# Normalising three layers by row tile and by half rows, the last layer's end written into both branches of a four-layer graph network

## The reference, cut to what matters

```python
edge_index = jnp.stack([src, dst])
x = _layernorm(x + _L0_gnn_ref(...))   # two RGCN layers, 3 relations, each with a gate over 8 x 64 query rows
x = _layernorm(x + _L1_gnn_ref(...))   # GCN: sum of (x @ W) over the edges, by degree, + b
x = _layernorm(x + _L2_gnn_ref(...))   # two RGAT layers with attention, 4 heads and 1 head
x = _layernorm(x + _L3_gnn_ref(...))   # RGCN with 34 relations, then a GCN: h1 @ W_gcn over the edges, + b_gcn

def _layernorm(x, axis=-1, eps=1e-05):
    m = jnp.mean(x, axis=axis, keepdims=True)
    v = jnp.var(x, axis=axis, keepdims=True)
    return (x - m) / jnp.sqrt(v + eps)
```

## Time and profile before

| | us |
|---|---|
| three timed runs | 1088.4, 1088.81, 1089.32 (median 1088.81) |
| the profiled execution | 1089.91 |
| its span, from the first to the last instruction | 1088.2 |
| its mean granted TensorE clock | 0.994 of full speed |
| TensorE busy | 1039.5 (96%) |
| VectorE busy | 764.1 (70%) |
| ScalarE busy | 573.4 (53%) |
| GpSimd busy | 263.4 (24%) |

### The profile page before, as it was taken

The page is one execution under the profiler, slowest core; times in us unless marked ns, Lnnn a source line. Parts: engine busy times, 40 slices in busy tenths (PEclk is TensorE's granted clock), DMA queues, the critical chain, the costliest instruction groups (busy, mean ns, idle before and its releaser), DMA issues.

```text
span 1088.2 us, 17713 instructions
## 1 busy us (share of the span) xinstructions
PE 1039.5 (96%) x7444; PEld 858.3 (79%) x7444; DVE 764.1 (70%) x1092; ACT 573.4 (53%) x606; POOL 263.4 (24%) x160
## 2 busy tenths in 40 slices
PE   6999999999999999999999989989999999999987
PEld 5889986454699984455879689956999999999974
DVE  8793855888654238887644584745989998989862
ACT  0432226888533248887324363324667676766630
POOL 3524705999300038996100000000000000000000
PEclk9999999999999999999999999999999999999999
DMA  8043247212043373220424302604978787877830
GB/s 296 12 135 129 88 149 230 59 59 59 2 174 123 119 220 130 60 59 20 160 88 175 117 1 87 246 11 138 304 256 283 256 284 256 270 261 263 276 118 29
DMA packets 82291, 163.18 MB, mean 150 GB/s; under 512 B 4044, under 2 KB 60136, under 8 KB 81918
## 3 DMA queue, kind: packets, MB, share of 16 engines
q1 hardware_dynamic: 80736, 151.86, 41.4%
q0 software_dynamic: 1472, 10.15, 3.4%
HBM read 158.35 MB, written 0.80 MB: 146 GB/s over the span
## 4 chain that ended last, share of the span: by engine, by line
PE 80%; DVE 13%; issue 4%; ACT 2%; POOL 1%; DVEq 0%; POOLq 0%; ACTq 0%
PE PS L1089 20%; PE PS L770 8%; PE PS L941 7%; PE PS L786 5%; PE PS L692 5%; PE PS L581 4%; PE PS L1072 4%; PE PS L511 4%; PE PS L668 4%; PE PS L524 3%; PE PS L593 3%; PE PS L1105 2%; PE PS L1006 2%; PE PS L828 2%; DVE PRD L1677 1%
## 5 line engine op out<-in xcount | busy, mean ns | idle before, releaser
L1926 DVE TENSOR_TENSOR Wlo<-W,Whi 128x2304 fp32r<-128x2304 f32 x68 | 172.1, 2551 | 19.0 <-ACT Whi L1425 19.0
L1425 ACT CAST Whi<-W 128x2304 fp32r<-128x2304 f32 x68 | 144.5, 2127 | 0.2 <-DMA W<-in_L_rel 0.2
L1089 PE MATMUL PS<-Whi,Mhi 128*128 128x384 f32 x408 | 138.0, 338 | 0.0
L1089 PE MATMUL PS<-Wlo,Mhi 128*128 128x384 f32 x408 | 136.5, 335 | 0.0
L1089 PE MATMUL PS<-Whi,Mlo 128*128 128x384 f32 x408 | 136.5, 334 | 0.0
L478 POOL TENSOR_TENSOR PRDP<-arena 128x1024 f32<-128x1024 f32 x48 | 114.8, 2391 | 30.1 <-issue 17.9
L770 PE MATMUL PS<-QH,SEL 128*128 128x512 f32 x384 | 115.7, 422 | 5.3 <-ACT xT L1262 1.4
L1283 ACT ACTIVATE arena<-PS 128x1024 f32<-128x1024 f32 x96 | 98.4, 1025 | 23.6 <-PE PS L770 23.5
L770 PEld LDWEIGHTS PS<-QH,SEL 128*128 128x128 f32 x384 | 64.8, 188 | 55.2 <-DVE PRD L1677 21.3
L1283 ACT ACTIVATE PS<-PS 128x1024 f32<-128x1024 f32 x96 | 97.9, 1019 | 2.6 <-PE PS L770 2.6
L1089 PEld LDWEIGHTS PS<-Whi,Mhi 128*128 128x128 f32 x408 | 76.8, 188 | 0.4 <-DVE Wlo L1926 0.2
(11 more groups left out here) (296 smaller groups left out, 2430.3 us busy)
## 6 DMA issues: line engine op xcount, KB each, us to landing
W<-in_L_rel SPq DMA_DIRECT2D x68, 1152.0 KB, 6.4
W<-in_W_rel SPq DMA_DIRECT2D x6, 2304.0 KB, 9.3
W<-in_W SPq DMA_DIRECT2D x6, 2304.0 KB, 9.4
arena<-in_qU SPq DMA_DIRECT2D x96, 128.0 KB, 2.6
W<-in_WqT SPq DMA_DIRECT2D x4, 2304.0 KB, 9.7
W<-in_W_root SPq DMA_DIRECT2D x2, 2304.0 KB, 13.5
W<-in_WgT SPq DMA_DIRECT2D x2, 2304.0 KB, 9.7
QH<-QH POOLq DMA_DIRECT2D x2, 1536.0 KB, 9.9
```

Source lines behind the costliest of these rows:

```text
L1089: mm = pe.matmul(PS[:, 4 + s % 2, 0:HALF], MS[a][mb][:, k, j * P:(j + 1) * P], WS[b][w % 3][:, k, :], start=n == 0, stop=n == 17)
L1425: nc.scalar.copy(WS[0][w % 3][:], W[(FIRST34 + r) % 2][:, :, q * HALF:(q + 1) * HALF]).then_inc(w_hi, 1)
L1926: V.tensor_tensor(WS[1][w % 3][:], W[(FIRST34 + r) % 2][:, :, q * HALF:(q + 1) * HALF], WS[0][w % 3][:].bitcast(F32), ALU.subtract).then_i ...
```

## The change

1. `norm_x`, `normalise`: normalisations 2, 3 and 4 go by row tile. `normalise_tile(n, t)` makes mean and variance of one tile, waits for ScalarE's root of that tile (128x1 in place of 128x2), and scales that tile. It stands right behind the statistics of its tile. Normalisation 1 keeps its form as `normalise_first`. The counts that engines wait for follow.
2. `gcn_out` adds the results of layers 1 and 3 by half rows: `natural` tells `rows_done` after each of its first three halves, VectorE adds one half (128x384) and takes its statistics. `row_stats` goes.
3. The rows are turned tile by tile: tile 0 right behind the product (after 4 warm-up products in layer 1, none in layer 2), then 16 warm-up products, then tile 1. Before, 26 and 18 stood ahead of both. After layer 2 the turned rows go to banks 4 to 6 in place of 0 to 2.
4. The end of layer 3 (`last_product` on TensorE, `last_rows` on VectorE) is written into both branches in place of once behind them. ScalarE's end stays behind its branches.
5. ScalarE takes a square root of `eps` into an unused tile `eps_sd`, ahead of its wait for the turned counts.

```diff
-            def natural(bank, T, Wm, first=True, last=True, ready=None, tile_sem=None):
+            def natural(bank, T, Wm, first=True, last=True, ready=None, half_sem=None):
                 for t in range(NT):
-                    if t and tile_sem:
-                        mm.then_inc(tile_sem, 1)
                     for h in range(2):
+                        if half_sem and (t, h) != (0, 0):
+                            mm.then_inc(half_sem, 1)
...
-            def to_turned(bank, N, ready=None):
+            def to_turned(bank, N, ready=None, between=None):
                 for t in range(NT):
+                    if t and between:
+                        between()
...
-            natural(4, hT, W[m % 2], ready=sums_ready(1), tile_sem=rows_done).then_inc(w_used, 1)
-            keep_busy(26, 3)
+            natural(4, hT, W[m % 2], ready=sums_ready(1), half_sem=rows_done).then_inc(w_used, 1)
+            keep_busy(4, 3)
...
-            to_turned(0, xN, ready=lambda t: pe.wait_ge(ln_done, 2 + t + 1)).then_inc(x_turned, 1)
+            to_turned(0, xN, ready=lambda t: pe.wait_ge(ln_done, 2 + t + 1), between=lambda: keep_busy(16, 3)).then_inc(x_turned, 1)
...
-            keep_busy(18, 7)
-            to_turned(0, xN, ready=lambda t: pe.wait_ge(ln_done, 2 * 2 + t + 1)).then_inc(x_turned, 1)
+            to_turned(4, xN, ready=lambda t: pe.wait_ge(ln_done, 2 * 2 + t + 1), between=lambda: keep_busy(16, 7)).then_inc(x_turned, 1)
...
+            def last_product():
+
+                keep_busy(10, 7)
+                gcn_sums(2)
+                m = FIRST34 + R34
+                pe.wait_ge(w_in[m % 2], 16 * (FIRST34 // 2 + 1))
+                natural(0, hT, W[m % 2], ready=sums_ready(2), half_sem=rows_done).then_inc(w_used, 1)
...
                 scatter(PAIRS34 - 1, (3,)).then_inc(enc_done, 1)
+                last_product()
             with pe.Else():
...
                 pe.sem_inc(enc_done, 1)
-            keep_busy(10, 7)
-            gcn_sums(2)
-            m = FIRST34 + R34
-            pe.wait_ge(w_in[m % 2], 16 * (FIRST34 // 2 + 1))
-            natural(0, hT, W[m % 2], ready=sums_ready(2), tile_sem=rows_done).then_inc(w_used, 1)
+                last_product()
...
             def norm_x(n):
-                act.wait_ge(var_ready, n)
-                nc.scalar.activation(sd[:], mv[:, :, 1], ACT.Sqrt, bias=eps[:, 0:1]).then_inc(sd_ready, 1)
+                if n == 1:
+                    act.wait_ge(var_ready, 1)
+                    nc.scalar.activation(sd[:], mv[:, :, 1], ACT.Sqrt, bias=eps[:, 0:1]).then_inc(sd_ready, 1)
+                    return
+                for t in range(NT):
+                    act.wait_ge(var_ready, 2 * n - 2 + t)
+                    nc.scalar.activation(sd[:, t:t + 1], mv[:, t, 1:2], ACT.Sqrt, bias=eps[:, 0:1]).then_inc(sd_ready, 1)
...
+            nc.scalar.activation(eps_sd[:], eps[:], ACT.Sqrt)
             act.wait_ge(cn_turned, 1)
...
+            def normalise_tile(n, t):
+
+                V.bn_aggr(mv[:, t, :], stats[:, t, :, :]).then_inc(var_ready, 1)
+                dve.wait_ge(sd_ready, 2 * n - 2 + t)
+                then(V.reciprocal(rstd[:, t:t + 1], sd[:, t:t + 1]))
+                V.tensor_scalar(xN[:, t, :], xN[:, t, :], mv[:, t, 0:1], rstd[:, t:t + 1], ALU.subtract, ALU.mult).then_inc(ln_done, 1)
+                if t == NT - 1:
+                    dve.wait_ge(ln_done, 2 * n)
...
-                    if t == 0:
-                        dve.wait_ge(rows_done, n)
-                    else:
-                        dve.wait_ge(w_used, 16 if n == 1 else FIRST34 + 1)
-                    xv = xN[:, t, :].rearrange("p (h f) -> p h f", h=2)
-                    then(V.scalar_tensor_tensor(out=xv, in0=PS[:, 4 - sums_bank(n) + 2 * t:6 - sums_bank(n) + 2 * t, 0:HALF], scalar=dinv[:, t:t + 1], in1=xv,
-                                                op0=ALU.mult, op1=ALU.add))
-                    row_stats(t)
+                    for h in range(2):
+                        if t == h == 1:
+                            dve.wait_ge(w_used, 16 if n == 1 else FIRST34 + 1)
+                        else:
+                            dve.wait_ge(rows_done, 3 * (n - 1) + 2 * t + h + 1)
+                        xv = xN[:, t, h * HALF:(h + 1) * HALF]
+                        then(V.scalar_tensor_tensor(out=xv, in0=PS[:, 4 - sums_bank(n) + 2 * t + h, 0:HALF], scalar=dinv[:, t:t + 1], in1=xv,
+                                                    op0=ALU.mult, op1=ALU.add))
+                        ins = V.bn_stats(stats[:, t, h, :], xv)
+                    then(ins)
+                    normalise_tile(2 * n, t)
...
             middle_sums(1)
             gcn_out(1, 1)
-            normalise(2)
...
                             ins = V.bn_stats(stats[:, t, part, :], xv)
-                    then(ins)
+                        then(ins)
+                        normalise_tile(3, t)
                 u0 += 2 * H
-            normalise(3)
...
                 rows_lo(2 * R34 - 1)
+                last_rows()
+            steps[0] = before
             with dve.Else():
...
                 normalise34(R34 - 1, 1)
+                last_rows()
```

More of the change, by code:

```diff
@@ L1316, in turn_x @@
                 for j in (0, 2):
-                    nc.scalar.copy(xT[:, 2 * j:2 * j + 2, :], PS[:, j, :].rearrange("p (k n) -> p k n", k=2)).then_inc(xT_ready, 1)
+                    nc.scalar.copy(xT[:, 2 * j:2 * j + 2, :], PS[:, 4 + j, :].rearrange("p (k n) -> p k n", k=2)).then_inc(xT_ready, 1)
             def sums_out(n):
@@ L1736, in _, with normalise_first @@
                             third_lo_turned(3 * p + 4)
-            def row_stats(t):
-                for h in range(2):
-                    ins = V.bn_stats(stats[:, t, h, :], xN[:, t, h * HALF:(h + 1) * HALF])
-                then(ins)
-            def normalise(n):
+            def normalise_first():
                 for t in range(NT):
@@ L1748, in normalise @@
                 ins.then_inc(var_ready, 1)
-                dve.wait_ge(sd_ready, n)
+                dve.wait_ge(sd_ready, 1)
                 then(V.reciprocal(rstd[:], sd[:]))
-                if n == 1:
-                    dve.wait_ge(dinv_ready, 1)
-                    then(V.tensor_tensor(scaled_rstd[:], rstd[:], dinv[:], ALU.mult))
-                    for t in range(NT):
-                        V.tensor_scalar(hN[:, t, :], xN[:, t, :], mv[:, t, 0:1], scaled_rstd[:, t:t + 1], ALU.subtract, ALU.mult
-                                        ).then_inc(gcn_scaled, 1)
+                dve.wait_ge(dinv_ready, 1)
+                then(V.tensor_tensor(scaled_rstd[:], rstd[:], dinv[:], ALU.mult))
+                for t in range(NT):
+                    V.tensor_scalar(hN[:, t, :], xN[:, t, :], mv[:, t, 0:1], scaled_rstd[:, t:t + 1], ALU.subtract, ALU.mult
+                                    ).then_inc(gcn_scaled, 1)
                 for t in range(NT):
                     V.tensor_scalar(xN[:, t, :], xN[:, t, :], mv[:, t, 0:1], rstd[:, t:t + 1], ALU.subtract, ALU.mult).then_inc(ln_done, 1)
-                dve.wait_ge(ln_done, 2 * n)
+                dve.wait_ge(ln_done, 2)
+            def normalise_tile(n, t):
[5 more added lines that the diff above has]
+                    dve.wait_ge(ln_done, 2 * n)
             def middle_sums(n):
@@ L1984, in normalise34, with last_rows @@
                 V.tensor_tensor(N34[j], A34[j], RC[:, 1, :].unsqueeze(1).to_broadcast([P, NT, NODES]), ALU.mult).then_inc(nrm_ready, 1)
+            def last_rows():
+                dve.wait_ge(w_used, FIRST34)
+                for t in range(NT):
+                    ins = V.tensor_scalar(BR[:, t, :], biasN[:, 4, :], dinv[:, t:t + 1], None, ALU.mult)
+                ins.then_inc(bias_scaled, 1)
+                dve.wait_ge(enc_done, 1)
+                dve.wait_ge(bias_scaled, 1)
+                for t in range(NT):
+                    V.scalar_tensor_tensor(out=hN[:, t, :].rearrange("p (h f) -> p h f", h=2), in0=PS[:, 2 * t:2 * t + 2, 0:HALF],
+                                           scalar=dinv[:, t:t + 1], in1=BR[:, t, :].rearrange("p (h f) -> p h f", h=2),
+                                           op0=ALU.mult, op1=ALU.add).then_inc(gcn_scaled, 1)
+                middle_sums(2)
+                gcn_out(2, 0)
             dve.wait_ge(slots_in, 16)
+            before = steps[0]
             overflow = dve.value_load(flag[0:1, 0:1])
@@ L2034, in _ @@
                 normalise34(R34 - 1, 1)
-            dve.wait_ge(w_used, FIRST34)
-            for t in range(NT):
-                ins = V.tensor_scalar(BR[:, t, :], biasN[:, 4, :], dinv[:, t:t + 1], None, ALU.mult)
-            ins.then_inc(bias_scaled, 1)
-            dve.wait_ge(enc_done, 1)
-            dve.wait_ge(bias_scaled, 1)
-            for t in range(NT):
-                V.scalar_tensor_tensor(out=hN[:, t, :].rearrange("p (h f) -> p h f", h=2), in0=PS[:, 2 * t:2 * t + 2, 0:HALF],
```

(6 more changed lines are left out.)

5 lines of the change are left out of this document (3 added, 2 removed).

## The result

| | before | after |
|---|---|---|
| timed runs, us | 1088.02 to 1089.32, median 1088.61 (4) | 1082.24 to 1083.07, median 1082.51 (4) |
| ratio, with its 95% interval | | 0.9942 [0.9929, 0.9954] |
| profiled execution, us | 1089.91 | 1082.61 |
| its span | 1088.2 | 1080.9 |
| TensorE busy | 1039.5 (96%) | 1038.2 (96%) |

The kernel became faster by 6.3 us by the ratio (6.1 by the medians). The forecast was 1079.9 us, so it is 2.6 us short; the time lies inside the range given, 1078.6 to 1082.8. Each place that the prediction summed gained nearly what was forecast. What is missing lies where it gave nothing: in the last store, as the traces show, and, as far as they can tell, in a stretch of layer 2.

The account below looks back on a forecast made before the run. TensorE was taken to bound the kernel, so VectorE's work pays only where TensorE stands still. 0.44 + 1.60 + 0.90 + 4.39 + 1.58 = 8.91 us off the 1088.81 median gives 1079.9 us; range 1078.6 to 1082.8.

Parts of the forecast that it names:

- The three places: Layer 1 into 2, layer 2 into 3, and the end: where normalisations stand between two pieces of TensorE's work.
- carried through to the end: Layer 3's long loop: TensorE's alone, untouched by the change, so a gain ahead of it reaches the end.
- middle stretch: From layer 2's first products to its last weighted sums; the forecast's sum has no term for it.
- The table: ScalarE's early table load, drawn into an idle gap before its copy; first root then waits for VectorE alone: 0.44 us.
- Place A: Layer 1 into layer 2: rows normalised in halves, so layer 2's products start sooner: 1.60 us, 1.3 if transposes take longer.
- Place B: Layer 2 into layer 3: one scaling and six transposes less between weighted sums and next product: 0.90 us.
- Place C: Layer 3's end, in both branches: no jump before the last product and no fall of the clock: 4.39 us.
- the stall: Rival at the end: TensorE's 3.31 us of standing is no jump and stays; 1084.3 us, chance 0.07.
- VectorE's gap of 1.26 us: Rival at the end: VectorE's gap before the scaled rows comes again in copied code; 1081.1 to 1082.2 us, chance 0.11.
- stall for a fetch: Rival in layer 3's loop: moved code makes TensorE stand at block ends, 3.31 us each; chance 0.04.
- The last rows: From the last product's end to the last scaled row, by halves: 1.58 us.
- The store: Final store: SyncE's 2.4 us wait stays, 0 to 0.6 better taken as 0; VectorE's jump at most 0.3, taken as 0.

Follow-up runs that it names:

- the best version: Changed kernel with VectorE's last jump under the last product, weight split earlier, 11 warm-ups for 16, turned banks told singly: 1080.63 us, again 1080.42 us.
- the end in both branches alone: Kernel before with only layer 3's end written into both branches, nothing else of the change: 1086.69 us, ratio 0.9973.
- the jump under the last product: Changed kernel, but VectorE's final adding and normalising stand once behind both branches, its copied end going only to the bias: 1081.88 us, ratio 0.9935.
- A held back: Changed kernel with 30 in place of 16 warm-up products ahead of tile 1's turning between layers 1 and 2: 1084.34 us, ratio 0.9956.
- the end once: Changed kernel with layer 3's end (last product and last rows) once behind both branches, as before the change: 1086.44 us, ratio 0.9977.

## Why the prediction was right, and where it was short

**What bounds the kernel.** The three places were the right ones, and the trace after has TensorE standing less in each. The sentence that a gain ahead of the loop "is carried through to the end" held for layer 3: from the root's product to the last scatter's end are 319.5 us in both traces. It was said of the loop alone, though A's gain also has the middle stretch to cross, which the prediction didn't read. There 1.2 to 1.3 us are given back in six of seven traces with a short A and the warm-ups unchanged, and in none of the three with A at 6.87 or 6.88. This step failed, by what the traces show; the pair of traces with the result has no such loss (149.29 and 149.27).

**The table.** 0.44 forecast, 0.44 measured. The root of eps took 0.20, inside the 0.30 allowed.

**Place A.** 1.60 forecast, 1.61 measured, by the same chain; the scaling was to end 2.74 us after the product and ends at 560.46, 2.73 after it. The lower bound of 1.3 wasn't needed.

**Place B.** 0.90 forecast, 0.74 measured. The mis-sized term is the six transposes, put at half of 1.54 = 0.77: they take 0.89. The mean and variance of one tile take 0.22, not 0.18. (The prediction's own terms add up to 733.31 and not 733.35, a gain of 0.94.)

**Place C.** 4.39 forecast, 4.43 measured in the traces and 4.56 between the two kernels that differ in nothing else. Both halves came, stall and clock. The rivals fall here: the stall didn't stay, VectorE's gap of 1.26 us is not there in the copied code, and no stall for a fetch shows in the loop: from the root's product to the last scatter it took the same 319.5 us.

**The last rows.** 1.58 forecast, 1.60 measured up to the last row.

**The store.** This step failed too: the wait "stays", 0 to 0.6 us better, "taken as 0", and VectorE's jump "at most some 0.3 us", "taken as 0". The wait became 3.0 and 3.3 in place of 2.4. The prediction asked whether VectorE would be done before the store is, and took for the store the 3.2 us of before, where two stores shared the way; a single one without the jump has the span's end 2.77 us behind the row, and VectorE's jump lasts 3.2 (1077.1 to 1080.3). So the jump was mis-sized by itself, some 0.8 us by these rows where at most 0.3 was allowed. Nor did the prediction ask what the jump does to the store, though it says that no transfer is moved past another: code is fetched in the same microseconds. The Trainium skill's "Runtime: NRT & Kernel Launch", section "Instruction fetch mechanics", says that a taken branch to code outside the loaded pages forces a DMA fetch of it; the packet on an instruction queue while the store is under way, gone without the jump, agrees. Without the jump a lone store waits 2.0, so the bound of 0.6 better was nearly right (0.4), and it was the jump that took it away.

**The rest.** Of the 2.6 us missing, 0.16 are B, 0.6 to 0.9 the store, and up to 1.3 the middle stretch: 2.0 to 2.4. The mean granted clock of the plain runs speaks for the last, but weakly. The fall of 3.40 us at half the clock in place C (rows 9) is 0.0016 of the mean of a whole execution, so its end should have raised that mean; it is 0.9944 over 63 runs of the kernel before beside the experiments, and 0.9946 over the 10 of the kernel after. But the mean also counts a fall behind the last product, where no product is left to be slowed: within the span 3.06 and 2.65 us in the two traces of before, 4.33 and 3.07 in those of after, 1.56 and 1.52 in those of the best version. That is 0.0004 of the missing rise, and most of the best version's higher mean (0.9959 over 10 runs). Some 0.0010 is left, about 2 us at half the clock in an average execution, which came back somewhere; the mean doesn't tell where.

**What stays open.** Why the middle stretch is longer mostly when A is short isn't settled. The traces show one thing more: of the eleven traces with its warm-ups unchanged, the five in which the fall begins 55.3 to 55.9 us behind layer 2's first product have it for 6.8 us, the four in which it begins at 56.2 to 57.2 for 3.41 (after, both of before, the end in both branches alone). The other two are long in another way: with the jump under the last product the one fall of 3.41 begins at 65.1, over work that counts, and with A held back there are two of 3.41, at 57.6 and 64.5. With A at 6.87 or 6.88 the earliest begins at 56.8. What sets the beginning was not measured. Plain executions have no traces, so that the middle is where they lose is inferred. The last few tenths are within the scatter of single runs (1085.92 to 1092.2 for the kernel before).

## What to carry to other kernels

A chain read step by step, with every hand-over counted, gives the gain of a place to 0.2 us; the error lay in what the place hands on to, in the store for certain and in the middle stretch by inference, so follow a gain across each later stretch where TensorE's clock falls, and take its length there from more than one trace. Ask of every jump that moves not only whether its engine has time, but which transfer is under way when its code is fetched. Here the jump belongs under the last product, where nothing waits for VectorE or for the DMA engines, and not under the last store.

## What the runs showed of the hardware

- A jump over the other branch costs TensorE 3.2 to 3.3 us with no releaser named (3.31 before, 3.16 in the end once), with one block of code fetched in it. VectorE's jump at its end held VectorE for 3.2 us (1077.1 to 1080.3), and beside it a 384 KB store landed after 3.4 us in place of 2.3.
- The same instruction stream had falls of the granted clock to 0.50 of 3.41 us in one execution and 6.82 us in another, starting 56.2 and 55.5 us behind layer 2's first product. With products of 8 rows set between warm-ups a fall lasted 17.05 us, although TensorE counted as busy in all of it.
- The six transposes took 0.89 us alone; twelve in a row took 1.54.
